# Depthwise layer: vertical taps in three fp32r passes, horizontal sums in PSUM, 3x3 branch as ScalarE products added by GpSimd, stores by chunk

## The reference

```python
x_33 = dwconv(x, w0, b0)                                  # 3x3
x_15 = dwconv(dwconv(x, w0_1, b0_1), w0_2, b0_2)          # 1x5, then 5x1
x_111 = dwconv(dwconv(x, w1_1, b1_1), w1_2, b1_2)         # 1x11, then 11x1
add = x_33 + x_15 + x_111
mixer = einsum('nchw,oc->nohw', add, w3) + b3
return mixer * x
```

## Time and profile before

| What | us |
|---|---|
| median of 3 runs (range) | 6795.28 (6787.41 to 6802.78) |
| the profiled execution's own time | 6799.16 |
| its span | 6797.1 |
| VectorE busy, whole span | 4483.5 (66%) |
| TensorE busy, whole span | 5450.1 (80%) |
| GpSimd busy, whole span | 2301.0 (34%) |
| ScalarE busy, whole span | 2062.3 (30%) |

### The profile page before, as it was taken

One profiled execution on the slowest core, in us unless ns is written; L12 is line 12 of the kernel. 1 busy time (PEld: TensorE's weight loads), 2 busy tenths in 40 slices (PEclk: granted clock), 3 DMA queues, 4 the chain that ended last, 5 costly groups with the idle time before them and its releaser, 6 DMA issues. The chain is left out here.

```text
span 6797.1 us, 125088 instructions
## 1 busy us (share of the span) xinstructions
PE 5450.1 (80%) x48621; PEld 4102.8 (60%) x48621; DVE 4483.5 (66%) x7316; ACT 2062.3 (30%) x3979; POOL 2301.0 (34%) x1228
## 2 busy tenths in 40 slices
PE   3878787878787785195775969999969999999991
PEld 2646555555555463174564824444459999999991
DVE  5766766766667675687787589999933333455553
ACT  2656565666556563132222212111100000000000
POOL 1544354544535353274665534554400000000000
PEclk9989898989888897597988979999979999999995
DMA  3000000000000001232221101001030000000005
GB/s 127 15 27 27 27 17 24 22 19 27 14 27 14 27 15 48 63 97 68 80 86 54 47 29 50 25 25 50 12 137 0 0 0 0 0 0 0 0 0 185
DMA packets 78550, 251.90 MB, mean 37 GB/s; under 512 B 25248, under 2 KB 26528, under 8 KB 67872
## 3 DMA queue, kind: packets, MB, share of 16 engines
q1 hardware_dynamic: 78112, 246.07, 10.5%
HBM read 139.49 MB, written 67.11 MB: 30 GB/s over the span
## 5 line engine op out<-in xcount | busy, mean ns | idle before, releaser
L2198 DVE SCALAR_TENSOR_TENSOR l_state<-l_conv,l_state 128x256 f32 x500 | 292.7, 585 | 783.3 <-PE l_conv L2134 783.3
L517 POOL TENSOR_TENSOR l_probs<-l_probs,l_inv 128x1024 f32<-128x1024 f32 x256 | 495.6, 1940 | 625.3 <-DVE l_inv L926 624.7
L1900 PE MATMUL l_mix<-l_mid,l_fold 128*128 128x512 f32 x1408 | 632.2, 606 | 79.0 <-DVE l_mid L1996 78.7
L1428 PE MATMUL l_gather_ps<-l_wdiag,l_stage 128*128 128x128 f32 x4608 | 547.1, 279 | 163.9 <-DVE l_wdiag L1583 163.8
L1428 PEld LDWEIGHTS l_gather_ps<-l_wdiag,l_stage 128*128 128x128 f32 x4608 | 537.1, 195 | 208.0 <-issue 150.1
L1996 DVE SCALAR_TENSOR_TENSOR l_mid<-l_xpad,l_w,l_mid 128x1024 f32<-128x1024 f32 x448 | 635.7, 1441 | 2.3
L2134 PE MATMUL l_conv<-l_carry_hi,l_taps_lo 128*128 128x248 f32 (+2 forms) x4500 | 624.8, 284 | 0.0
L2134 PE MATMUL l_conv<-l_carry_hi,l_taps_hi 128*128 128x248 f32 (+2 forms) x4500 | 621.8, 282 | 2.9 <-DVE l_carry_hi L2164 2.0
L2134 PE MATMUL l_conv<-l_carry_lo,l_taps_hi 128*128 128x248 f32 (+2 forms) x4500 | 619.6, 282 | 0.0
L2134 PEld LDWEIGHTS l_conv<-l_carry_hi,l_taps_lo 128*128 128x128 f32 x4500 | 577.9, 190 | 0.0
L2134 PEld LDWEIGHTS l_conv<-l_carry_hi,l_taps_hi 128*128 128x128 f32 x4500 | 575.6, 189 | 3.3 <-DVE l_carry_hi L2164 2.2
(11 more groups left out here) (267 smaller groups left out, 8880.2 us busy)
## 6 DMA issues: line engine op xcount, KB each, us to landing
l_xleft<-l_xt SPq DMA_DIRECT2D x64, 283.5 KB
l_xright<-l_xt SPq DMA_DIRECT2D x64, 283.5 KB
stat_xs<-in_x SPq DMA_DIRECT2D x8, 2048.0 KB, 23.2
l_hats<-in_x SPq DMA_DIRECT2D x8, 2048.0 KB, 7.6
l_xraw<-in_x SPq DMA_DIRECT2D x8, 2048.0 KB, 9.0
after_layer<-l_xraw SPq DMA_DIRECT2D x64, 256.0 KB, 2.0
l_xblk<-after_layer SPq DMA_DIRECT2D x32, 512.0 KB, 4.6
l_xres<-after_layer SPq DMA_DIRECT2D x32, 512.0 KB, 4.3
```

Source lines behind the costliest of these rows:

```text
L517: pool.tensor_tensor(part, part, inv[:, u, cols].rearrange("c (j o) -> c j o", o=1).to_broadcast([C, 4, KEYS]), ALU.mult).then_inc(scaled_ ...
L1428: last = pe.matmul(gather_ps[u][y // 4][:, y % 4 * C:(y % 4 + 1) * C], stage[:, u, y + k // 3, :], wdiag[:, y % SLOTS, k, :], start=(k == ...
L1900: pe.matmul(bank[:, :], fold11[:, j, :], flat(mid11[:, r + j:r + j + ROWS, :]), start=(j == 0), stop=False)
L2198: dve.scalar_tensor_tensor(row, conv[h][:, 0:HB * W].rearrange("c (b w) -> c b w", b=HB), 0.0, row, op0=ALU.max, op1=ALU.add).then_inc(lin ...
```

## The change

- The horizontal sums of the 1 x 11 and 1 x 5 branches are accumulated in PSUM (`acc11`, `acc5`, one block each), the first tap by ScalarE, the others by VectorE. The chains are no longer interleaved: all of 11, then all of 5.
- Each finished sum is split in two parts in fp32r, a reduced form of fp32 of which the layer behind (layer 3) makes use already: ScalarE copies the sum into `hi11` or `hi5`, which rounds it, and VectorE subtracts that from the sum into `lo11` or `lo5`. The folded weights are split likewise, once.
- TensorE does the vertical taps in three passes (hi x hi, hi x low weights, lo x hi): 48 fp32r matmuls per chunk instead of 16 fp32 ones, and the fp32 one for `sum33` as before.
- The 3 x 3 branch leaves VectorE. ScalarE writes the first tap into `sum33` and the eight other products into three buffers `prod33` in turn; GpSimd adds them one by one. Products 0 to 2 of a block wait until all eight adds of the block before are done, a later product j until add j - 3 is.
- Evacuation and gate run five chunks behind the block in work (`LAG`), statistics seven, both placed inside the block.
- `res` is one buffer for one batch, and each chunk is stored by a DMA of its own (256 KB).

The core of the diff, empty lines left out:

```diff
...
+    BLOCK = BROWS * W
...
+    LAG = 5
+    ADDS, PRODUCTS = 8, 3
...
-        mid5 = mem.sbuf("mid5", [C, H + 2 * P5, W])
-        mid11 = mem.sbuf("mid11", [C, H + 2 * P11, W])
-        res = mem.sbuf("res", [C, 2, HW])
+        hi5 = mem.sbuf("hi5", [C, H + 2 * P5, W], FP32R)
+        lo5 = mem.sbuf("lo5", [C, H + 2 * P5, W], FP32R)
+        hi11 = mem.sbuf("hi11", [C, H + 2 * P11, W], FP32R)
+        lo11 = mem.sbuf("lo11", [C, H + 2 * P11, W], FP32R)
+        res = mem.sbuf("res", [C, CHUNKS, CHUNK])
+        prod33 = mem.sbuf("prod33", [C, PRODUCTS, BLOCK])
...
+        fold = sum33[:, :, :].rearrange("c h w -> c (h w)")[:, 0:FOLDS * C].rearrange("c (k o) -> c k o", o=C)
+        fold_hi = mem.sbuf("fold_hi", [C, FOLDS, C], FP32R)
+        fold_lo = mem.sbuf("fold_lo", [C, FOLDS, C], FP32R)
...
+        acc11 = mem.psum("acc11", (C, BLOCK))
+        acc5 = mem.psum("acc5", (C, BLOCK))
...
+        def behind(i, s, blk, lag):
+            for c in (2 * blk - lag, 2 * blk - lag + 1):
+                n, k = s + c // CHUNKS, c % CHUNKS
+                if not isinstance(i, int) or i * 2 + n >= 0:
+                    yield i + n // 2, n % 2, k
...
-                n = i * 2 + s
-                sp.wait_ge(res_ready, (n + 1) * CHUNKS)
-                sp.dma_start(out[bass.ds(n, 1)].rearrange("b c n -> (b c) n"), res[:, s, :]).then_inc(stored[s], 16)
+                for k in range(CHUNKS):
+                    sp.wait_ge(res_ready, count(i, s, CHUNKS, k + 1))
+                    at = out[bass.ds(i * 2 + s, 1)].rearrange("b c n -> (b c) n")
+                    sp.dma_start(at[:, k * CHUNK:(k + 1) * CHUNK], res[:, k, :]).then_inc(stored[k], 16)
...
+            def add33(i, s, blk, *products):
+                for j in products:
+                    pool.wait_ge(made33, count(i, s, BLOCKS * ADDS, blk * ADDS + j + 1))
+                    if j:
+                        pool.wait_ge(added33, count(i, s, BLOCKS * ADDS, blk * ADDS + j))
+                    else:
+                        pool.wait_ge(first33, count(i, s, BLOCKS, blk + 1))
+                    pool.tensor_tensor(part33(blk), part33(blk), rows(prod33[:, j % PRODUCTS, :]), ALU.add).then_inc(added33, 1)
...
+            def gate(i, s, k):
+                pool.wait_ge(evacuated, count(i, s, CHUNKS, k + 1))
+                image = rows(res[:, k, :])
+                pool.tensor_tensor(image, image, interior(s, k * ROWS, ROWS), ALU.mult).then_inc(gated, 1)
+                pool.wait_ge(gated, count(i, s, CHUNKS, k + 1))
+                pool.tensor_tensor(res[:, k, :], res[:, k, :], xin[:, s, k * CHUNK:(k + 1) * CHUNK], ALU.add).then_inc(res_ready, 1)
...
+            def batch(i, s):
+                for blk in range(BLOCKS):
+                    due = list(behind(i, s, blk, LAG))
+                    add33(i, s, blk, 0, 1, 2)
+                    for j, t, k in due[:1]:
+                        gate(j, t, k)
+                    add33(i, s, blk, 3, 4)
+                    for j, t, k in due[1:]:
+                        gate(j, t, k)
+                    add33(i, s, blk, 5, 6, 7)
...
+            def chunk(i, s, k):
+                need = min(BLOCKS - 1, (k * ROWS + ROWS - 1 + P11) // BROWS)
+                pe.wait_ge(lo5_done, count(i, s, BLOCKS, need + 1))
+                pe.wait_ge(added33, count(i, s, BLOCKS * ADDS, ADDS * (k // 2 + 1)))
+                wait(pe, evacuated, count(i, s, CHUNKS, k + 1 - NPS))
+                bank = mix[k % NPS]
+                r = k * ROWS
+                pe.matmul(bank[:, :], w3T[:, :], flat(sum33[:, r:r + ROWS, :]), start=True, stop=False)
+                for p, (weights, five, eleven) in enumerate(((fold_hi, hi5, hi11), (fold_lo, hi5, hi11), (fold_hi, lo5, lo11))):
+                    for j in range(11):
+                        last = pe.matmul(bank[:, :], weights[:, 5 + j, :], flat(eleven[:, r + j:r + j + ROWS, :]), start=False, stop=False)
+                    for j in range(5):
+                        last = pe.matmul(bank[:, :], weights[:, j, :], flat(five[:, r + j:r + j + ROWS, :]), start=False,
+                                         stop=(p == 2 and j == 4))
+                last.then_inc(mixed, 1)
...
+            def firsts(i, s, blk):
+                tap, src = taps_of_11(s, blk)[0]
+                wait(act, lo11_done, count(i, s, BLOCKS, blk))
+                act.activation(rows(acc11[:, :]), src, ACT.Identity, scale=tap, bias=biases[:, 3:4]).then_inc(first11, 1)
+                tap, src = taps_of_5(s, blk)[0]
+                wait(act, lo5_done, count(i, s, BLOCKS, blk))
+                act.activation(rows(acc5[:, :]), src, ACT.Identity, scale=tap, bias=biases[:, 1:2]).then_inc(first5, 1)
+                tap, src = taps_of_33(s, blk)[0]
+                wait(act, mixed, count(i, s, CHUNKS, 2 * blk + 2 - CHUNKS))
+                act.activation(part33(blk), src, ACT.Identity, scale=tap).then_inc(first33, 1)
...
+            def products33(i, s, blk, *products):
+                for j in products:
+                    tap, src = taps_of_33(s, blk)[j + 1]
+                    before = blk * ADDS + j + 1 - PRODUCTS
+                    if j < PRODUCTS:
+                        before = blk * ADDS
+                    wait(act, added33, count(i, s, BLOCKS * ADDS, before))
+                    act.activation(rows(prod33[:, j % PRODUCTS, :]), src, ACT.Identity, scale=tap).then_inc(made33, 1)
...
+            def evacuate(i, s, k):
+                act.wait_ge(mixed, count(i, s, CHUNKS, k + 1))
+                wait(act, stored[k], count(i, s, 16, 0))
+                wait(act, stats_done, count(i, s, CHUNKS, k + 1 - CHUNKS))
+                act.activation(res[:, k, :], mix[k % NPS][:, :], ACT.Identity, bias=mix_bias[:, :]).then_inc(evacuated, 1)
...
+            def high11(i, s, blk):
+                wait(act, mixed, count(i, s, CHUNKS, chunks_read(blk) - CHUNKS))
+                act.wait_ge(taps11_done, count(i, s, BLOCKS, blk + 1))
+                act.activation(part11(hi11, blk), rows(acc11[:, :]), ACT.Copy).then_inc(hi11_done, 1)
...
+            def high5(i, s, blk):
+                act.wait_ge(taps5_done, count(i, s, BLOCKS, blk + 1))
+                act.activation(part5(hi5, blk), rows(acc5[:, :]), ACT.Copy).then_inc(hi5_done, 1)
...
+            def batch(i, s, last=False):
+                for blk in range(BLOCKS):
+                    if blk == 0:
+                        act.wait_ge(normed[s], i + 1)
+                    firsts(i, s, blk)
+                    products33(i, s, blk, 0, 1, 2)
+                    for j, t, k in behind(i, s, blk, LAG):
+                        evacuate(j, t, k)
+                    if blk == BLOCKS - 1 and not last:
+                        norm(i + s, 1 - s)
+                    products33(i, s, blk, 3, 4)
+                    high11(i, s, blk)
+                    products33(i, s, blk, 5)
+                    high5(i, s, blk)
+                    products33(i, s, blk, 6, 7)
...
+            act.wait_ge(fold_made, 1)
+            act.activation(fold_hi[:, :, :], fold, ACT.Copy).then_inc(fold_hi_made, 1)
...
+            act.wait_ge(folds_ready, 1)
...
+            dve.wait_ge(fold_made, 1)
+            dve.wait_ge(fold_hi_made, 1)
+            dve.tensor_tensor(fold_lo[:, :, :], fold, fold_hi[:, :, :], ALU.subtract).then_inc(folds_ready, 1)
...
+            def sum_taps(i, s, blk, acc, taps, before, first, done):
+                dve.wait_ge(first, count(i, s, BLOCKS, blk + 1))
+                for j in range(1, len(taps)):
+                    tap, src = taps[j]
+                    if j > 1:
+                        dve.wait_ge(tap_chain, count(i, s, BLOCKS * 12, before + j - 1))
+                    last = dve.scalar_tensor_tensor(acc, src, tap, acc, op0=ALU.mult, op1=ALU.add)
+                    if j < len(taps) - 1:
+                        last.then_inc(tap_chain, 1)
+                last.then_inc(done, 1)
...
+                    sum_taps(i, s, blk, rows(acc11[:, :]), taps_of_11(s, blk), 12 * blk, first11, taps11_done)
+                    sum_taps(i, s, blk, rows(acc5[:, :]), taps_of_5(s, blk), 12 * blk + 9, first5, taps5_done)
+                    dve.wait_ge(hi11_done, count(i, s, BLOCKS, blk + 1))
+                    dve.tensor_tensor(part11(lo11, blk), rows(acc11[:, :]), part11(hi11, blk), ALU.subtract).then_inc(lo11_done, 1)
+                    for j, t, k in behind(i, s, blk, LAG + 2):
+                        stats(j, t, k)
+                    dve.wait_ge(hi5_done, count(i, s, BLOCKS, blk + 1))
+                    dve.tensor_tensor(part5(lo5, blk), rows(acc5[:, :]), part5(hi5, blk), ALU.subtract).then_inc(lo5_done, 1)
...
```

More of the change, by code:

```diff
@@ L1859, in _ @@
             pool.memset(xpad[:, :, :, :], 0.0).then_inc(pads_zero, 1)
[L1860 to L1864, removed]
-                for s in range(2):
[L1866 to L1873, removed]
```

(59 more changed lines are left out.)

154 lines of the change are left out of this document (66 added, 88 removed).

## The result

The changed kernel takes 6639.74 us (median of 4 runs, 6626.67 to 6642.55) against 6791.34 us (4 runs) before: ratio 0.9771, interval 0.9752 to 0.9791. The forecast was 6604 us, range 6545 to 6690: the sign, the bounding engine and the range held, but the gain is 152 us and not 187.

The account below looks back on a forecast made before the run. GpSimd's adds were to bound each block at 25.4 us; start, three blocks at 22.9, 28 periods and the tail end the layer at 4782.2, a gain of 191 us from 6799.2, hence 6604 us (median), range 6545 to 6690.

Parts of the forecast that it names:

- The signs: Marks of being right: adds 2.34 to 2.36 us, GpSimd above 90% busy, TensorE some 93%, VectorE 85 to 90%.
- The main question: Whether GpSimd's adds and gates run at their minima, 2.34, 1.18 and 1.26 us, beside the new VectorE instructions; taken as yes.
- the first rival: GpSimd still held up, losing 0.87 us on each of 12 instructions per block: period 35.8 us, time 6909 us; 10%.
- the second rival: Slow PSUM accumulation on VectorE: 1.62 us per chained tap, loop 27.1 us, 60 us more, 6664 us; 10%.
- Plain adds of 1.90 us: Rival: GpSimd's adds cost 1.90 us, its period is 21.9, TensorE's 23.6 bounds, 50 us less, 6554 us; 8%.
- the clock: Rival: TensorE held at a lower clock, mean 0.85 against 0.98 granted; its 23.6 us become 27.8, time 6671 us; 7%.
- three blocks without full gates: Start of the depthwise layer: three blocks run at VectorE's 22.9 us each, before the GpSimd-paced periods.
- 28 periods: Main loop of the layer to the last block's first add: 28 blocks at GpSimd's 25.4 us each.
- My own case: GpSimd's chain of adds paces the layer, time from 6585 to 6635 us; 63%.
- the gap: Between blocks GpSimd idles 1.3 us, since product 0 of the next block waits for all eight adds.
- The 0.08: Time in us from a GpSimd instruction's end to the start of one waiting for it; seven per block, 0.56 us.
- The stores by chunk hold nobody: Eight store issues of some 0.35 us per batch on SP delay no engine; last store falls from 7.3 to 2.0 us.

Follow-up runs that it names:

- one pass: Changed kernel with only the first of the three vertical passes, the products with the low parts left out: 6616.08 us.
- both edits: Changed kernel with four product buffers, each product waiting only for its own buffer, and the gate operations placed between the adds: 6579.91 us, ratio 0.9682.
- both, one pass: Kernel with four product buffers and gates between the adds, running only the first of the three vertical passes: 6550.08 us.
- The fp32 kernel: Changed kernel with the vertical taps as 16 fp32 products a chunk in one pass, low parts made but not read: 6736.0 us.

## Why the prediction was right, and where it was short

**Bound and sign: right, and shown.** GpSimd's adds pace the layer: taking its wait away and reordering its queue each shortened the block by what the chain says, taking two thirds of TensorE's vertical matmuls away gave 0.4 us a block. The signs agree in the main: GpSimd is busy 91%, TensorE 94%, and ScalarE waits most for the adds (277.1 us). Two do not: the adds take 2.40 us and not 2.34 to 2.36, and VectorE is busy 81% and not 85 to 90.

**The main question, whether GpSimd runs unhindered: right.** The gates fell to 1.20 and 1.29 us. With the 11-tap sums back in SBUF the hindrance returned on both engines, so it is the PSUM sums that remove it; the first rival had the mechanism, the place of the sums decides it. These rows agree with the Trainium skill's rule that I weighed ("SBUF — State Buffer", section Who interferes with whom).

**PSUM accumulation: right.** 18.38 us for 14 taps against 18.2; the second rival is out. Plain adds of 1.90 us are out too (2.40), and the clock stayed at 0.98.

**The size.** Term by term, from the profiled execution:

| stretch | predicted, us | measured, us |
|---|---|---|
| layer's first instruction to the first add | 32.0 | 31.8 |
| three blocks without full gates | 68.7 | 70.0 |
| 28 periods | 28 x 25.4 = 711.2 | 736.0 (26.29 each) |
| last block's first add to the next part | 55.0 | 57.8 |

My own case was to end between 6585 and 6635 us; 6639.74 lies 5 above that, inside the outer range alone. The sum is 28.7 too short, and 24.8 of it is one step: "Busy: 8 x 2.34 + 2 x (1.18 + 1.26) = 23.6; with 0.56, 24.2", and 1.3 for the gap. The adds measure 2.40 (+0.5), the gates 1.20 and 1.29 (+0.1), an add's start behind its predecessor 0.155 and not 0.08 (+0.4 over five), less 0.16 for four instructions that don't depend on theirs and start 0.04 early, and the gap 1.37 (+0.1). The 0.08 came from a gate's pair of 512 elements, and I put it on adds that no row showed in a chain. The gap itself was sized right, but it belongs to the wait as it is written and not to three buffers as such. In the last stretch chunks 5, 6 and 7 start 0.8 us earlier than predicted and take TensorE 38.0 us (4772.88 to 4810.92) for 35.5. One part is the matmul: 0.228 per fp32r matmul was too little, 0.234 was within my bounds, and a chunk in a steady stream takes 12.05 to 12.14 for 11.8. The other is the first of the three: it comes after 1.82 us of waiting, the granted clock is 0.67 between 4772.80 and 4778.00, and it takes 13.77. From the last matmul to the next part are 6.9 us for 5.8. Another 7 us lie outside the layer: this execution came to it 6.9 us later than the profiled one of before (3922.19 and 3915.27), through the same code.

**Stores.** "The stores by chunk hold nobody" was right, but I gave them the tail alone. With one result buffer they are worth about 62 us in time; the price of a whole store was nowhere in the sum.

**The rule against the change.** "GPSIMD Engine Reference", section Engine selection, in the Trainium skill would keep the 3x3 branch on VectorE. An add on GpSimd is indeed twice a tap, but on VectorE the branch makes the kernel 6932 us, 292 more: what counts is which engine has room.

**What stays open.** Why the adds grow from 2.35 to 2.40 us (below), and whether three product buffers with a narrower wait would do what four do.

## What to carry to other kernels

When work moves to an engine that was idle, take its durations from rows where the neighbours run as they will, and its spacing from a chain of the same kind: 0.06 and 0.08 us on each of some ten instructions were most of this miss. In an engine's queue put independent instructions between those that read each other's result, and let the first product of a round start as soon as its own buffer is free, so that it is ready when the last one is used; here a fourth buffer and a wait by buffer did that together. When two engines stand 0.2 us a block apart, look at both for idle time before shortening either: in the version with both edits, TensorE had none left. Where a result buffer is single, count who stands behind the instruction that waits for the store, not only the store.

## What the runs showed of the hardware

- A GpSimd add of 1024 elements takes longer in the kernels with more fp32r matmul records: 2.35 us while TensorE is idle (three in 7.35 us at 3953.98), 2.369 at 140 records in 100 us (one pass), 2.374 at 154 (both, one pass), 2.400 at 380 (changed kernel), 2.406 at 417 (both). The fp32 kernel does not fit between them: 235 longer records, TensorE busy 100%, and 2.360. So neither the number of records nor TensorE's busy share gives the order in all kernels, and the mechanism is not shown.
- On GpSimd, reading the result of the instruction just ahead costs 0.20 us for 1024 elements and 0.12 for 512, against an independent successor.
- When VectorE reads two SBUF operands beside a GpSimd instruction, VectorE loses as well as GpSimd: its 1.28 us become 3.32 or 2.11, GpSimd's add of 2.40 us becomes 3.31. With the sum in PSUM neither loses: 14 taps in 18.38 us, adds of 2.40.
